# Cross-attention and feed-forward kernel on one core: the two weight buffers of the feed-forward products 32 bytes further in each partition

## The reference

```python
x = x + attention(layernorm(x), ctx, Wq, Wk, Wv, Wo)     # x 16x112x1024, ctx 16x375x1024, 32 heads, 8 key/value heads
n = layernorm(x).reshape(1792, 1024)
g = n_quantised @ dequant(w1).T                          # 3584 columns
u = n_quantised @ dequant(w3).T                          # 3584 columns
h = silu(g) * u
x = x + h_quantised @ dequant(w2).T                      # back to 1024
```

## Time and profile before

| | |
|---|---|
| Three executions | 2510.83 us median (2504.62 to 2513.42) |
| The profiled execution | span 2511.5 us from its first to its last instruction; no other time of it is given |
| TensorE, matmuls | 2424.5 us, 97% of the span |
| Weight loads, beside them | 2069.3 us, 82% |
| VectorE | 1727.6 us, 69% |
| ScalarE | 979.1 us, 39% |
| GpSimd | 576.1 us, 23% |
| DMA | 162 GB/s over the span |

### The profile page before, as it was taken

The page is one execution under the profiler, slowest core; times in us unless marked ns, Lnnn a source line. Parts: engine busy times, 40 slices in busy tenths (PEclk is TensorE's granted clock), DMA queues, the critical chain, the costliest instruction groups (busy, mean ns, idle before and its releaser), DMA issues.

```text
span 2511.5 us, 35414 instructions
## 1 busy us (share of the span) xinstructions
PE 2424.5 (97%) x12682; PEld 2069.3 (82%) x12682; DVE 1727.6 (69%) x2639; ACT 979.1 (39%) x1673; POOL 576.1 (23%) x305
## 2 busy tenths in 40 slices
PE   7998999999999699799999999999999989999999
PEld 7997878878876388699999988998899978888887
DVE  6425777777776446788888889898889874445442
ACT  3212445444454422444444445344443342323221
POOL 1000354454454400011111111332333320000000
PEclk9998999999998799899999999999999999999999
DMA  7534555455545345465655554666676687565652
GB/s 225 174 96 135 146 135 146 131 142 143 133 113 130 86 155 168 126 203 168 186 170 168 165 151 148 181 180 183 194 211 182 172 284 228 170 186 151 186 163 84
DMA packets 369146, 408.04 MB, mean 162 GB/s; under 512 B 125824, under 2 KB 324096, under 8 KB 359152
## 3 DMA queue, kind: packets, MB, share of 16 engines
q1 hardware_dynamic: 369008, 406.22, 56.7%
HBM read 252.99 MB, written 152.70 MB: 162 GB/s over the span
## 4 chain that ended last, share of the span: by engine, by line
PE 44%; DVE 9%; issue 3%; DMA 2%; ACT 0%; DVEq 0%; ACTq 0%
PE bank L84 15%; PE bank L85 15%; PE bank L86 15%; DVE g_WL L90 2%; DMA stash<-weight_scratch 2%; DVE g_su L1731 1%; DVE stash L1736 1%; DVE g_XL L90 1%; DVE stash L1228 1%; DVE stash L1226 1%; DVE xT L1723 1%; DVE stash L1225 1%; DVE stash L1249 0%; ACT g_XH L1659 0%; ACT g_WH L1198 0%
## 5 line engine op out<-in xcount | busy, mean ns | idle before, releaser
L84 PE MATMUL bank<-g_XH,g_WH 128*128 128x448 f32 (+1 forms) x2254 | 847.1, 376 | 30.2 <-DVE g_XL L90 15.9
L86 PE MATMUL bank<-g_XH,g_WL 128*128 128x448 f32 (+1 forms) x2254 | 845.0, 375 | 0.0
L85 PE MATMUL bank<-g_XL,g_WH 128*128 128x448 f32 (+1 forms) x2254 | 844.9, 375 | 0.0
L84 PEld LDWEIGHTS bank<-g_XH,g_WH 128*128 128x128 f32 x2254 | 424.5, 188 | 93.7 <-DVE g_WL L90 18.1
L86 PEld LDWEIGHTS bank<-g_XH,g_WL 128*128 128x128 f32 x2254 | 424.6, 188 | 55.3
L85 PEld LDWEIGHTS bank<-g_XL,g_WH 128*128 128x128 f32 x2254 | 424.7, 188 | 54.3
L90 DVE TENSOR_TENSOR g_WL<-stash,g_WH 128x512 fp32r<-128x512 f32 (+1 forms) x417 | 349.3, 841 | 75.8 <-ACT g_WH L1198 47.1
L1198 ACT ACTIVATE g_WH<-stash 128x512 fp32r<-128x512 f32 x392 | 241.7, 628 | 398.9 <-PE bank L86 245.1
L696 DVE TENSOR_REDUCE a_nm<-bank 112x1 f32<-112x375 f32 x512 | 264.9, 531 | 117.1 <-PE bank L831 113.8
L800 ACT ACTIVATE a_pr<-bank 125x448 f32<-125x448 f32 x384 | 204.0, 545 | 204.4 <-PE bank L907 150.8
L649 POOL TENSOR_TENSOR a_prsum<-a_pr 125x1792 f32<-125x1792 f32 x32 | 129.3, 4042 | 363.0 <-ACT a_pr L800 363.0
(11 more groups left out here) (132 smaller groups left out, 3617.8 us busy)
## 6 DMA issues: line engine op xcount, KB each, us to landing
stash<-in_L_ffn_w SPq DMA_DIRECT2D x168, 256.0 KB, 5.2
weight_scratch<-stash SPq DMA_DIRECT2D x28, 1024.0 KB, 7.6
stash<-weight_scratch SPq DMA_DIRECT2D x28, 1024.0 KB, 5.4
h_scratch<-g_Sh SPq DMA_DIRECT2D x112, 224.0 KB, 2.8
down_scratch<-xT SPq DMA_DIRECT2D x98, 256.0 KB, 3.0
stash<-in_ctx SPq DMA_DIRECT2D x48, 500.0 KB
stash<-h_scratch SPq DMA_DIRECT2D x25, 896.0 KB, 6.4
a_qst<-q_scratch SPq DMA_DIRECT2D x96, 224.0 KB, 4.7
```

What stands on the lines that cost most here:

```text
L84: pe.matmul(acc, lh, rh, start=first, stop=False, skip_group_check=onto)
L85: pe.matmul(acc, lh, rl, start=False, stop=False, skip_group_check=onto)
L86: return pe.matmul(acc, ll, rh, start=False, stop=last, skip_group_check=onto)
```

## The change

A buffer of 8 elements (32 bytes) is placed ahead of `g_WH` and one of 24 elements (96 bytes) behind `g_WL`. Nothing reads or writes either.

```diff
+                sb("lead", [P, 8])
                 WH, WL = sb("WH", [P, 7, KH, P], f32r), sb("WL", [P, 7, KH, P], f32r)
+                sb("gap", [P, 24])
                 t1 = sb("t1", [P, KH, TB])
```

## The result

The change makes the kernel slower: 2521.07 us median of six runs (2519.31 to 2524.68) against 2510.42 us of six of the kernel before (2502.25 to 2513.42), a ratio of 1.0054 with a 95% interval of 1.004 to 1.0068 (the quotient of the two medians is 1.0042). It lies within the range of the prediction, on the side opposite to its forecast.

The account below looks back on a forecast made before the run. TensorE's pace of matmul starts was taken as the bound. From 2511.5 us, 26 gained in hidden products, 0 for down product and VectorE/ScalarE, 2 taken back gave 2487.5, stated as 2487 us; range 2478 to 2532.

Parts of the forecast that it names:

- What bounds the kernel: Feed-forward hidden and down products: for 1,445 of 2511.5 us TensorE's pace of starting matmuls sets the time.
- Step 1: Hidden products, 448 columns: differing 64-byte halves bring the query projection's 200.0 ns pace, gaining 26 us.
- Step 2: Down product, 512 columns: no change taken, 0 us; bounds no gain to a 13 us loss.
- Step 3: VectorE and ScalarE accesses to moved buffers: 0 us on the path, at most 6 us without room.
- Step 4: Hidden products at 200 ns: VectorE's share rises to 89%, its stalls take back 2 us.
- The start of the sum: Whole kernel: the profiled span of 2511.5 us from which the predicted gain was subtracted.
- Only the moving operand's place counts: Hidden and down products: moving blocks keep their place, so paces stay and time is 2511 us; chance 0.28.
- The down product pays: Down product loses 6.5 ns per matmul, 13 us, against the hidden products' 24 us gain: 2500 us; chance 0.07.
- The new relation is the worse one: Both products: weight blocks touching nine 64-byte pieces delay matmuls about 3 ns each, 20 us: 2531 us; chance 0.25.
- The value product: Attention part, 256 columns: slice times with shifted weights, 0.35 or 0.36 us, cited for no effect and for a loss.

Follow-up runs that it names:

- offset 64: Kernel before with a 16-element pad behind `WL`: moving operands start 64 bytes further relative to the weights (remainder by 256); 2506.41 us, executed once.
- the pad of 160: Kernel before with a 40-element pad behind `WL`, moving operands 160 bytes further, weights in place; 2511.27 us against 2505.2, ratio 1.0029.
- the re-profiled kernel: Kernel before, unchanged, profiled once more; 2502.45 us, span 2500.7 against 2511.5 us in the first profile.
- The last version: Kernel before with a 16-element pad behind `WL` and the down product's ring begun 48 elements later; 2496.66 us against 2505.77, ratio 0.9962.
- the first four runs: Against the kernel before: moving operands 32 bytes further, both operands shifted, only down weights shifted, only hidden weights shifted; ratios 1.0058, 1.0044, 1.0024, 1.0047.
- the two kernels at 128: Kernel before with weights 32 and moving operands 160 bytes further, 2517.76 us; or only moving operands 128 bytes further, 2518.22 us.
- the two mixed rows of the table: Kernel before with larger weight buffers, high and low weights at different distances: only down weights shifted, 2511.65 us; only hidden weights shifted, 2517.72 us.

## Why the prediction was wrong

- **What bounds the kernel** was right. Both stages go by the pace of starts; the result is made of 2,058 steps that each take 6.6 ns longer, with no wait added. That weights and moving data interact was right as well: in the down product moving either one changes the pace (the change and the run with the moving operands 32 bytes further), moving both together does not.
- **Step 1 failed**, "If what counts is whether they agree, the change makes them differ by moving the other one, and the pace goes to 200.0." I took 64 bytes for the unit of agreement. Nothing in the rows gave that unit; it came from having written every address against a multiple of 64. The runs contradict it both ways: at offset 64 the halves agree and the pace is 200.0 ns after every start, at 96 they differ and it is 205.3. Nor can the operands be exchanged: the query projection stands at offset 160 and the change at 96, which is 256 less 160, the same distance with weights and moving data exchanged, and yet the change has neither 200.0 nor 206.7 ns. Even the query projection's own offset would not have given its pace throughout, as the pad of 160 shows. The step was to give 26 us; it gave 205.3 ns, 0.4 ns under the profile of before. Against the re-profiled kernel's 203.4 ns it is even a loss, since offset 96 has lost the 202.7 ns pace too.
- **Step 2 failed in the choice between its bounds.** I took 0 because 13 ns is the least that any of the long streams lose, which speaks for no gain and says nothing of a loss. The other end, "at worst the same 6.5 ns come on top, 2,058 x 6.5 = 13 us", is what was measured (6.6 ns, 13.6 us). That no row showed 512 columns at another offset should have kept this end as likely as the other.
- **Step 3 held**: L90 on `g_WL` has a mean of 764 ns against 763:

```profile
L90 DVE TENSOR_TENSOR g_WL<-stash,g_WH 128x512 fp32r<-128x512 f32 x392 | 298.0, 764 | 54.5 <-ACT g_WH L1200 45.7
```

- **Step 4** could not be seen in the change, whose stage idles 14 us instead of 17. The last version shows its size: at 200.0 ns it takes back 9 us, where I had put 2. VectorE's share of 89% was computed rightly (865.95 of 976 us) and read wrongly: at that average TensorE's weight loads still waited for it 17 times, up to 4.5 us.
- **The start of the sum**, 2511.5 us, came from an execution in which only about a quarter of the hidden products had the 202.7 ns pace. In every run here the time lies 1.8 us above the span (2522.51 against 2520.7 us for the changed kernel), so that execution took some 2513 us, the highest of its three, and the second profile is 10.8 us shorter. This is no part of the failure, but it is as large as the effect itself.
- **The rivals.** "Only the moving operand's place counts" is refuted: the moving blocks kept their place within 128 bytes and the pace changed, while everything moved together changed nothing. "The down product pays" was right in its half of the sum and had the forecast's 200.0 ns in the other. "The new relation is the worse one" had the right sign but named the weights' own start, the ninth piece of 64 bytes, and the run with everything 32 bytes further has that and costs nothing.
- **The value product**, used on both sides, could decide nothing: from one slice to the next its weights go 1,504 bytes on, so the offset changes together with the start, which I had not taken into account.
- **The rule of the Trainium skill.** The Trainium skill, page "TensorE: Matmul & The Clock Gate", section "Step-by-step: what each phase is for", has the weight load on a read port of its own that takes no read bandwidth from the running matmul. The prediction concluded from it that the weights' place is worth nothing, and that does not hold for these fp32r products: 512 columns took from 226.7 to 234.3 ns with the offset between the two. The measurement decides; whether the loss arises in reading is not shown.

## What to carry to other kernels

Where TensorE never idles, divide a window by its number of matmuls, before and after. A pace that differs between two products of one shape is worth a trial with a pad; here the best placement found took 0.4% off the kernel. Write the addresses of both operands as a difference, look at its remainder by 256 bytes, and choose it by trial for each column count (of those tried, 64 was best for 448 columns, 0 and 256 for 512). When a pad is put in for an experiment, list what else it moves: three of the first four runs here changed the quantity that they were to keep.

## What was not expected of the hardware

- The pace of one product at one clock depends on the offset between moving block and weight block: 200.0 to 206.7 ns for 448 columns, 226.7 to 234.3 for 512.
- At offsets 0, 32 and 160, and in one of the two kernels at 128, the 448-column product takes more than one pace (a third one, 204.4 ns, once at 32) and keeps it for up to 2,015 matmuls. It changes at stalls, and in one case, at offset 160, without one. At 64 and 96 only one pace was seen. Between the two profiled executions of the kernel before this makes 10.7 of 10.8 us, so it can account for most of the spread of its runs, 2500 to 2513 us; those of the last version lie within 3.1 us.
- What goes on inside is not shown, and the offset does not settle everything: 128 came out in two ways (233.3 and 232.4 ns for 512 columns) with weights 32 bytes apart, 96 with its three values on other matmuls, and the two mixed rows of the table follow from no others. Offsets 192 and 224 were not tried.
